# A transformer layer with attention and experts: a unit's four part writes ahead of both of its stack fills on the sync engine

## The reference

```python
num = jnp.exp(jnp.einsum('bhqd,bhkd->bhqk', q_rot, k_rot) * scale)
den = jnp.sum(jnp.exp(jnp.einsum('bhqd,bhkd->bhqk', q, k) * scale), axis=-1, keepdims=True)
attn = jnp.where(causal[None, None], num / den, 0.0)
x = x + (attn @ v) @ Wout + bout
```

## Time and profile before

| | before |
|---|---|
| median of 3 runs | 1865.06 us (1864.2 to 1865.12) |
| the profiled execution, time | 1872.72 us |
| its span | 1871.0 us |
| mean granted TensorE clock | 0.941 |
| PE busy | 1549.3 us (83%) |
| ACT busy | 1601.1 us (86%) |
| DVE, POOL busy | 825.2 us (44%), 505.0 us (27%) |
| SyncE's DMA queue | 170.31 MB, 40.9% of 16 engines' span |

### The profile page before, as it was taken

One profiled execution on the slowest core, in us unless ns is written; L12 is line 12 of the kernel. 1 busy time (PEld: TensorE's weight loads), 2 busy tenths in 40 slices (PEclk: granted clock), 3 DMA queues, 4 the chain that ended last, 5 costly groups with the idle time before them and its releaser, 6 DMA issues.

```text
span 1871.0 us, 29149 instructions
## 1 busy us (share of the span) xinstructions
PE 1549.3 (83%) x8362; PEld 619.2 (33%) x8416; DVE 825.2 (44%) x1824; ACT 1601.1 (86%) x2633; POOL 505.0 (27%) x868
## 2 busy tenths in 40 slices
PE   3578988789788897888977887988978889778995
PEld 1222323233333333233332333323432333323333
DVE  4223433374334653355533644347423565235415
ACT  0589997899798997899978998989978999789990
POOL 3123232232232321333222313223123422124210
PEclk8799998999899998999989999999989999899986
DMA  4345433443544424454234545345254451444400
GB/s 117 77 102 116 93 88 67 94 110 72 125 101 90 111 53 102 100 124 102 63 88 97 121 86 117 84 94 115 61 108 102 103 120 39 99 102 94 102 23 23
DMA packets 88878, 172.40 MB, mean 92 GB/s; under 512 B 9344, under 2 KB 75904, under 8 KB 76416
## 3 DMA queue, kind: packets, MB, share of 16 engines
q1 hardware_dynamic: 88704, 170.31, 40.9%
HBM read 111.55 MB, written 58.72 MB: 91 GB/s over the span
## 4 chain that ended last, share of the span: by engine, by line
issue 32%; PE 26%; ACT 20%; POOL 9%; DVE 5%; DMA 5%; SPq 1%; DVEq 0%; ACTq 0%; POOLq 0%
ACT scores L463 13%; PE scores L505 7%; ACT probs L473 6%; PE y_ps L534 5%; PE scores L512 4%; POOL parts L386 4%; PE side L564 3%; DMA qk_parts<-parts 3%; POOL rot L384 2%; DMA stack<-qk_parts 2%; PE side L585 1%; POOL x_acc L414 1%; PE side L544 1%; SPq L313 1%; PE side L571 1%
## 5 line engine op out<-in xcount | busy, mean ns | idle before, releaser
L463 ACT ACTIVATE scores<-scores 128x1024 f32<-128x1024 f32 x1024 | 1046.6, 1028 | 23.9 <-PE scores L505 22.7
L473 ACT ACTIVATE probs<-scores 128x1024 f32<-128x1024 f32 x512 | 491.3, 1025 | 188.6 <-PE scores L512 186.7
L505 PE MATMUL scores<-stack 96*128 96x512 bf16 x2048 | 581.8, 385 | 59.2 <-ACT probs L473 25.5
L512 PE MATMUL scores<-stack 96*128 96x512 bf16 (+3 forms) x1536 | 345.2, 340 | 142.2 <-DMA stack<-qk_parts 123.1
L534 PE MATMUL y_ps<-probs,v_sb 128*32 128x512 f32 (+3 forms) x3072 | 331.3, 503 | 5.9 <-ACT probs L473 4.8
L376 POOL TENSOR_SCALAR_AFFINE_SELECT probs<-probs 128x256 f32<-128x256 f32 (+1 forms) x640 | 223.5, 375 | 372.6 <-ACT probs L473 218.5
L505 PEld LDWEIGHTS scores<-stack 96*128 96x128 bf16 x2048 | 161.2, 98 | 426.9 <-ACT scores L463 200.4
L512 PEld LDWEIGHTS scores<-stack 96*128 96x128 bf16 x1536 | 126.8, 100 | 420.6 <-issue 183.0
L384 POOL TENSOR_TENSOR rot<-raw,cos_sb 128x512 f32<-128x512 f32 x64 | 89.9, 1405 | 584.1 <-DVEq L831 584.1
L386 POOL TENSOR_TENSOR parts<-rest,parts 128x512 bf16<-128x512 f32 x128 | 147.7, 1154 | 343.5 <-DVE parts L818 337.2
L463 ACT ACTIVATION_READ_ACCUMULATOR scores<-scores 128x1 f32 x1024 | 205.5, 201 | 0.0
(11 more groups left out here) (110 smaller groups left out, 1123.6 us busy)
## 6 DMA issues: line engine op xcount, KB each, us to landing
qk_parts<-parts SPq DMA_DIRECT2D x128, 384.0 KB, 2.6
stack<-qk_parts SPq DMA_DIRECT2D x128, 384.0 KB, 6.3
stack<-qk_parts SPq DMA_DIRECT2D x128, 256.0 KB, 6.8
stack<-qk_parts SPq DMA_DIRECT2D x128, 128.0 KB, 7.6
x_in<-in_L_attn_x SPq DMA_DIRECT2D x8, 1024.0 KB, 5.4
out<-x_mid SPq DMA_DIRECT2D x32, 256.0 KB, 6.9
probs<-in_L_attn_Wqkv SPq DMA_DIRECT2D x1, 512.0 KB, 6.6
cos_sb<-in_cos SPq DMA_DIRECT2D x1, 512.0 KB, 7.3
```

The source lines that it names most:

```text
L463: nc.scalar.activation(src, src, ACT.Exp, scale=SCALE, accum_out=den[:, g % 2, i, j:j + 1]).then_inc(exp_done, 1)
L473: nc.scalar.activation(probs[:, chunk % 2, j, :], src, ACT.Exp, scale=SCALE).then_inc(exp_done, 1)
L505: mm = nc.tensor.matmul(tile[:, half * HALF:(half + 1) * HALF], q[:, j, i * P:(i + 1) * P], k[:, j, half * HALF:(half + 1) * HALF], start= ...
L512: mm = nc.tensor.matmul(tile[:, col:col + n], k[:, h, i * P:(i + 1) * P], q[:, h, q0:q0 + n], start=True, stop=True)
```

## The change

Within `send_parts` the two fills and the wait for `scores_ready` leave the loop over halves and kinds. They now follow it, so that all four writes of the unit are issued first, then the wait, then the plain fill and the rotated fill. The place of `send_out` in the loop stays as it was, so both output writes that go with a filling now come ahead of both fills.

```diff
                         sp.sem_inc(held["sp"], 1)
                         sp.dma_start(scratch[kind, :, :, :, half * HALF:(half + 1) * HALF].rearrange("c s r t -> (s r) c t"),
                                      parts[:, kind, :, :]).then_inc(sent, 16)
-                        if half == 1:
-                            if kind == 0 and not (isinstance(b, int) and b == 0 and g < 2):
-
-                                sp.wait_ge(scores_ready, at(b, G * NSTEP, (g - 1) * NSTEP))
-                                sp.sem_inc(held["sp"], 1)
-                            fill_stacks(b, g, kind, sent)
                     if outs is not None:
                         send_out(outs, half)
+                if not (isinstance(b, int) and b == 0 and g < 2):
+                    sp.wait_ge(scores_ready, at(b, G * NSTEP, (g - 1) * NSTEP))
+                    sp.sem_inc(held["sp"], 1)
+                for kind, sent in ((0, plain_sent), (1, rot_sent)):
+                    fill_stacks(b, g, kind, sent)
```

## The result

The change makes the kernel slightly slower: 1873.73 us (median of 15) against 1865.12 us, a ratio of 1.0042 with a 95% interval of 1.0031 to 1.0053. That is 8.6 us by the medians, where -2.8 us was forecast. The time lies in the stated range, but the sign is the other one.

A forecast was written before the change was run, and what follows sets the result against it. PE's waits for stack fills at first and second units bound the kernel; terms -2.4, -2.4 and +2.0 give -2.8 us on the profiled 1872.72, 1869.9, less 7.7 for the median: 1862.3 us, range 1853 to 1874.

The forecast's parts named there:

- rival (D): Starts of units do not feel the fills at all, so no difference, 1865 us; chance 0.04.
- Third price: The fourth write issued ahead of the two fills costs them 0.2 us, with 0 and 0.9 as bounds.
- the pair: Plain and rotated fill back to back, first issue to last landing: 11.4 + 8.7, plus 0.2 for the write: 20.3 us.
- First price: The plain fill starts later: 3.0 us at first units of batches 2 to 7, 3.7 at second units, 5.4 at batch 1.
- The old start: Before the change, at the turn to batch 2, the plain fill starts at 483.96; first issue to last landing 23.7 us.
- the sum: Later start plus new fill time less old, over the waiting turns: -2.8 us in all, -0.4 per first unit of batches 2 to 7.
- The first unit of batch 1: No outputs are sent yet and POOL's part is late; PE's start moves from 286.43 to 288.4, +2.0 us.
- The second units: Second unit of each batch: 3.7 + 20.3 - 24.2 = -0.2 us; taken as -0.3 eight times, -2.4 us.
- (A): Near balance at the 16 turns: two fills take 20.1 to 20.7 us, -6 to +4 us in all; chance 0.44.
- (C): Later plain-fill start at the 16 turns not paid back: two fills take 21.1 us, 12.8 us more, 1875; chance 0.24.
- the hole: Between a unit's two fills the queue runs low, 66 GB/s; about 3 us, to be gained by the change.
- (B): Queue runs better never empty: two fills take 19.4 us, 14.4 us less over 16 turns, 1848; chance 0.28.

The follow-up runs named there:

- the later start alone: The kernel before, but the plain fill also waits for POOL's fourth low part and the fourth write stays behind that fill: ratio 1.0285, median 1919.26 us.
- the second trace: The changed kernel run and profiled once more, unedited: ratio 1.0054 against the kernel before, median 1871.26 us, span 1869.2 us.
- the second trace of before: The kernel before, unchanged, profiled a second time: ratio 1.000, median 1860.21 us, profiled execution 1862.62 us.
- The kernel for the first units alone: The kernel before with the changed order only for the first unit of each batch, other units as before: ratio 1.0072.
- the closed hole alone: The kernel before with the fourth write issued between the two halves of the plain fill instead of behind the whole: ratio 0.9690, median 1808.32 us.

## Why the prediction was right or wrong, point by point

**Where the time is.** Right: PE's waits at first and second units. The third and fourth units add no loss. That the fills set these starts, which rival (D) denied, is shown by the later start alone: 3.3 us at each of 16 turns.

**Third price, and the pair.** The pair was put at 20.3 us. In the changed kernel's trace it is 21.0 and 19.1 in the two fillings shown; over the six first units with outputs 20.9 on average, over the eight second units 20.0. Over all 16 waiting turns it is 20.5, and 20.3 in the second trace, so the price itself was right on average. At the turn to batch 2 it lies just above the 20.9 at which the forecast called itself wrong. The Trainium skill's figure of bytes over 436 GB/s (DMA: Bandwidth & Descriptors, section Anatomy of one DMA) belongs there to DMAs that GpSimd issues; taken for the second of these fills, behind a first one of 11.4 us, the estimate is 15 us for the pair, and these runs deny it for such fills. The fourth write ahead of the reads lands in 2.6 to 3.1 us at 61 of the 64 fillings of the two traces, and in 4.1 at most, so the 2 us of HBM latency at high load that the Trainium skill names (same page, section Latency and other measured facts) did not appear.

**First price, the new start.** Right within 0.2 us: 1.03 us behind DVE's end (0.95 forecast), 0.81 behind POOL's (0.7).

**The old start: the step that failed.** The forecast took the plain fill's start at 483.96 and the turn's 23.7 us from one execution, and multiplied by six. That start followed a write that took 4.4 us to land, because an instruction packet crossed its end. In four traces 12 of 24 such writes land late and 12 in 2.6. The forecast's own gave 2.6 as the median and should have raised the question, and in its own trace one of the six turns, to batch 5, is a timely one. With 2.6 the old fill starts 2.84 us ahead of POOL's end instead of 1.07. Its price at a first unit is then, from the two kernels' traces: new start behind POOL's end 2.0 us, old start 2.8 ahead of it, so 4.8 us later; pair 20.9 instead of 24.3 (average of the six in the second trace of before). That is +1.4 us where the sum had -0.4. Where the write is late, the old lead is 1.0 and the old pair 23.8: 3.0 + 20.9 - 23.8 = +0.1. All traces together say it in three numbers: from POOL's last part to the last landing the twelve timely turns before take 21.4 us on average, the twelve late ones 22.7, and the twelve turns after 23.0. A timely turn thus loses 1.6 us and a late one 0.3. Over the six turns with half of them late that is +5.7 us, where the sum had -2.4; with none late, +9.6. The stalls ahead of ACT's first exponential of these units agree: 54.7 and 55.2 us in the two traces after, against 53.0, 46.1, 46.9 and 51.9 in the four before, +5.5 on average.

**The first unit of batch 1** was forecast as +2.0: its stall before ACT's first exponential grew from 6.4 to 8.5 us, +2.1. **The second units** were forecast as -2.4 in all: their stalls sum to 20.5 and 16.7 us in the two traces after, against 24.7, 22.5, 23.3 and 23.0 before, -4.8 on average. **The prologue's fill** was counted as 0: ACT starts its first unit at 68.3 us instead of 66.8, +1.5.

These sum to 5.7 + 2.1 - 4.8 + 1.5 = +4.5 us with half of the turns late, and +8.4 with none. Measured are 8.6 us by the medians and, between the mean spans of four traces before (1864.2) and two after (1870.0), 5.8; on the one chip that has traces of both, it is 1869.2 against 1860.0 and 1864.7, so 6.9. The kernel for the first units alone fits too: 9.6 + 2.1 + 1.5 = 13.2 us with none late, and its ratio of 1.0072 is 13.4. So the sign comes from the old start; up to 4 us of the size depend on how often the late landing occurs in executions without a profile, which no run here could tell, or have a cause that was not found.

**The rivals.** (A) had the pair right, 20.1 to 20.7 on average over the 16 turns, and the old start wrong. (C) had the place right: the later start is not paid back. It had the reason wrong, except at first units, where the pair comes near its 21.1: on average the hole was worth what I took, but the old start was earlier than in the trace I read. That the measured time is the one of (C) is therefore mostly luck. (B) is refused for this order: the pair is 20.5 and 20.3 on average, not 19.4, though single second units reach 18.3 to 19.3. Its gain was to be had in another order, however: the later start alone costs 2.85% and the closed hole alone gains 3.1%. In the change they nearly cancel, as forecast.

## What to carry to other kernels

When a change is the difference of two nearly equal prices at many turns, look at every turn and at more than one execution, and ask of each start whether what released it took its usual time; a writer's median on the page beside a longer one in the timeline is the sign. A blocked queue and a late start can be taken apart: send the small write that the next transfer waits for between the pieces of the large one, and neither is paid.

## What the runs showed of the hardware

A 384 KB write issued on POOL's queue behind all six DMAs of a fill on SyncE's queue (3.6 us after their start) moved its first packet 6.1 us later, when the fill's data were nearly through: 8.5 us to landing, where the same write behind the same fill on SyncE's own queue takes 8.3. Issued ahead of the last three of the six, its packets moved in turns with theirs and it landed 1.1 to 1.6 us before the fill's end. The same write lands in 2.6 us with an empty queue, and in 4.3 to 4.5 us at the 12 of 24 turns where a 16 KB instruction packet crosses its end.
